# A bidirectional-scan block between two attention blocks, one core: the scan's output projection and the second attention input stage as one pipeline over chunks

## What is computed

```
x  = x + 0.5 * ffn_ref(layernorm(x))                 # attention + experts, first time
x  = x + attn_ref(layernorm(x))                      # the scan block:
        y = scan_forward(..) + scan_reversed(..)     #   (512 channels per token)
        x = base + y @ out_proj_w.T                  #   output stage: 512 -> 256, plus the added row
x  = x + 0.5 * ffn_ref(layernorm(x))                 # second time; its input stage:
        t = (x - mean) / sqrt(var + 1e-5)            #   layernorm, kept for the residual
        a = t * rsqrt(mean(t*t) + 1e-6) * norm_w     #   rmsnorm
        q, k, v = a @ wq.T, a @ wk.T, a @ wv.T       #   256, 64 and 64 columns
```

## Time and profile before

| | |
|---|---|
| median of 3 runs | 8743.57 us (8741.03 to 8743.65) |
| profiled execution, its own time | 8750.53 us |
| its span, first to last instruction | 8748.8 us |
| mean granted TensorE clock | 0.950 of full speed |
| TensorE busy over the span | 84% |
| VectorE busy over the span | 86% |
| first DMA of `mamba_out` | 6207.32 us into the span |
| first q matmul of the second `ffn_in` | 6392.66 us |
| last v matmuls of the second `ffn_in` begin | 6522.91 us |

### The profile page before, as it was taken

The page is one execution under the profiler, slowest core; times in us unless marked ns, Lnnn a source line. Parts: engine busy times, 40 slices in busy tenths (PEclk is TensorE's granted clock), DMA queues, the critical chain, the costliest instruction groups (busy, mean ns, idle before and its releaser), DMA issues. The chain is left out here.

```text
span 8748.8 us, 137191 instructions
## 1 busy us (share of the span) xinstructions
PE 7384.9 (84%) x39098; PEld 2876.4 (33%) x39098; DVE 7557.3 (86%) x11017; ACT 5055.9 (58%) x7663; POOL 3676.0 (42%) x1812
## 2 busy tenths in 40 slices
PE   6788888889997888888878888888777888888799
PEld 3222222225543333333323333333542222222255
DVE  6898888878867999999979999999358988888888
ACT  3577777762235666666655555555224777777622
POOL 0010011100006999999969999999300100110000
PEclk8799999999999999999999999999987999999999
DMA  6001001012262222222223333333561011011122
GB/s 171 17 19 20 19 19 26 19 42 77 72 210 88 83 83 82 82 83 84 83 92 100 102 103 100 100 102 100 171 189 17 19 20 19 19 21 23 42 67 67
DMA packets 554170, 623.35 MB, mean 71 GB/s; under 512 B 205376, under 2 KB 363328, under 8 KB 549408
## 3 DMA queue, kind: packets, MB, share of 16 engines
q1 hardware_dynamic: 548896, 581.63, 22.8%
q0 software_dynamic: 4608, 33.56, 1.9%
HBM read 416.65 MB, written 163.76 MB: 66 GB/s over the span
## 5 line engine op out<-in xcount | busy, mean ns | idle before, releaser
L833 DVE TENSOR_REDUCE ffn_att_mx<-psum 128x1 f32<-128x512 f32 (+2 forms) x4840 | 2915.6, 655 | 389.7 <-PE psum L666 197.4
L794 ACT ACTIVATE ffn_att_e<-psum,unscale 128x1024 f32<-128x1024 f32 (+3 forms) x2560 | 2384.0, 983 | 843.9 <-PE psum L739 842.9
L632 POOL TENSOR_SCALAR_AFFINE_SELECT ffn_att_e<-ffn_att_e 128x512 f32<-128x512 f32 x512 | 324.6, 634 | 3125.8 <-ACT ffn_att_e L794 3125.8
L666 PE MATMUL psum<-ffn_att_k,ffn_att_q 48*128 48x512 f16 (+3 forms) x5384 | 989.1, 368 | 611.2 <-DVE ffn_att_mx L833 545.2
L1628 POOL TENSOR_TENSOR scan_r_h<-scan_r_h,scan_r_cs 128x1024 f32<-128x1024 f32 x512 | 1207.1, 2447 | 148.0 <-ACT scan_r_state L1791 144.7
L705 PE MATMUL psum<-ffn_att_e,ffn_att_v 128*32 128x512 f32 (+3 forms) x10240 | 1248.5, 558 | 10.0 <-issue 3.8
L1628 POOL TENSOR_TENSOR scan_f_h<-scan_f_h,scan_f_cs 128x1024 f32<-128x1024 f32 x512 | 1204.4, 2444 | 118.8 <-ACT scan_f_state L1791 116.1
L1707 PE MATMUL psum<-scan_f_h,ident 128*128 128x512 f32 x2048 | 989.0, 623 | 84.0 <-POOL scan_f_h L1628 83.1
L1707 PE MATMUL psum<-scan_r_h,ident 128*128 128x512 f32 x2048 | 975.0, 617 | 78.1 <-POOL scan_r_h L1628 77.5
L1831 ACT ACTIVATE psum<-scan_r_dt,scan_r_an 128x512 f32<-128x512 f32 x1024 | 698.1, 682 | 456.2 <-DVE scan_r_h L1923 456.0
L1831 ACT ACTIVATE psum<-scan_f_dt,scan_f_an 128x512 f32<-128x512 f32 x1024 | 697.6, 681 | 423.8 <-DVE scan_f_h L1923 423.3
(11 more groups left out here) (240 smaller groups left out, 9216.5 us busy)
## 6 DMA issues: line engine op xcount, KB each, us to landing
scan_f_cs<-scan_f_bcd SPq DMA_DIRECT2D x264, 256.0 KB, 3.2
scan_r_cs<-scan_r_bcd SPq DMA_DIRECT2D x264, 256.0 KB, 3.3
scan_f_bs<-scan_f_bcd SPq DMA_DIRECT2D x82, 256.0 KB, 3.5
scan_r_bs<-scan_r_bcd SPq DMA_DIRECT2D x82, 256.0 KB, 3.5
scan_f_win<-xp SPq DMA_DIRECT2D x18, 1036.0 KB, 6.6
scan_r_win<-xp SPq DMA_DIRECT2D x18, 1036.0 KB, 7.0
ffn_att_q<-q_parts SPq DMA_DIRECT2D x144, 128.0 KB, 2.9
mamba_out_ys<-yz SPq DMA_DIRECT2D x18, 1024.0 KB, 7.3
```

Source lines behind the costliest of these rows:

```text
L632: nc.gpsimd.affine_select(out=part, in_=part, compare_op=ALU.is_ge, fill=0.0, base=0, pattern=[[0, REP], [1, P]], channel_multiplier=-1).t ...
L666: ins = nc.tensor.matmul(psum[:, turns[hh], j * w:(j + 1) * w], q[at, i // HALF, pair, i % HALF * P:(i % HALF + 1) * P], k[at, c * P:c * P ...
L794: nc.scalar.activation(E[:, s % PB, 2 * hp:2 * hp + 2, off:CH], psum[:, 2 * hp:2 * hp + 2, off:CH], ACT.Exp, scale=unscale[:, 0:1]).then_i ...
L833: nc.vector.reduce_max(mx[:, hh * 2 + pairs[0]:hh * 2 + pairs[1], i // HALF, i % HALF, c // TT], psum[:, turn, 0:(pairs[1] - pairs[0]) * w ...
```

## The change

`mamba_out` is removed, and the second call of `ffn_in` with it. A new function `mamba_out_ffn_in` does the work of both in one phase. The first call of `ffn_in` is as before. In the new phase the added rows are written into `xs` and go on from there to the statistics; they are still stored to `x2`, which `ffn_out` reads, and no longer loaded by the input stage. TensorE does out_project(i+2) between q(i) and turn(i+1), into PSUM banks 6 and 7 for even and odd chunks alike. VectorE does join(i+2) and statistics(i+2) between the q remainder and the k remainder of chunk i; ScalarE takes root(i+2) at the end of its step, no longer before the k copy. SP loads `wo` first. Its first DMAs of a step are the store of `t`(i+1), then behind both halves of join(i+2) the store of the rows and the loads of chunk i+4, then the stores of q, k and v. The steps 14 and 15 have no out_project and no join.

```diff
-def mamba_out(nc, tag, psum, y_in, base, x_out, outT, n_chunks):
+def mamba_out_ffn_in(nc, tag, psum, ident, spread, y_in, base, outT, x_out, t_out, qp, kp, v_out, w_norm, wqT, wkT, wvT, B, S):
...
+                def load(i, par):
+                    sp.dma_start(ys[par][:, :, :], cols(y_in, i)).then_inc(loaded[par], 16)
+                    sp.dma_start(bs[par][:, :, :], rows(base, i)).then_inc(loaded[par], 16)
...
+                sp.dma_start(wo[:, :, :], outT.rearrange("(m p) n -> p m n", p=P)).then_inc(wo_in, 16)
+                load(0, 0)
+                load(1, 1)
...
+                for i in range(2):
+                    sp.wait_ge(joined, 2 * (i + 1))
+                    store_x(i, i)
+                    load((i + 2) % n_chunks, i)
+                    if i == 0:
+                        sp.wait_ge(t_ready, TT)
+                        store_t(0, 0)
...
+                    if nxt:
+                        sp.wait_ge(t_ready, TT * (i + 2))
+                        store_t(i + 1, 1 - par)
+                    if more:
+                        sp.wait_ge(joined, 2 * (i + 3))
+                        store_x(i + 2, par)
+                        load((i + 4) % n_chunks, par)
+                    sp.wait_ge(high, 2 * (i + 1))
+                    store_part(0)
+                    sp.wait_ge(v_ready, i + 1)
+                    sp.dma_start(rows(v_out, i), vs[par][:, :, :]).then_inc(stored[par], 16)
+                    sp.wait_ge(low, 2 * (i + 1))
+                    store_part(1)
...
+                def join(i, par):
+                    dve.wait_ge(loaded[par], 32 * (i // 2 + 1))
+                    dve.wait_ge(x_stored[par], 16 * (i // 2))
+                    for n in range(2):
+                        dve.wait_ge(o_ps, 2 * i + n + 1)
+                        nc.vector.tensor_tensor(xs[par][:, 2 * n:2 * n + 2, :], psum[:, 6 + n, :].rearrange("p (t c) -> p t c", t=2),
+                                                bs[par][:, 2 * n:2 * n + 2, :], ALU.add).then_inc(joined, 1)
...
+                def statistics(i, par):
+                    dve.wait_ge(joined, 2 * (i + 1))
...
+                join(0, 0)
+                statistics(0, 0)
+                norm(0, 0)
+                join(1, 1)
+                statistics(1, 1)
+
+                def step(i, par, nxt, more):
+                    if nxt:
+                        norm(i + 1, 1 - par)
+                    split_low_q(i, par)
+                    if more:
+                        join(i + 2, par)
+                        statistics(i + 2, par)
+                    split_low_k(i, par)
...
+                def out_project(i, par):
                     pe.wait_ge(loaded[par], 32 * (i // 2 + 1))
-                    pe.wait_ge(added, 2 * i)
+                    pe.wait_ge(joined, 2 * i)
                     for t in range(TT):
                         for m in range(DM):
-                            ins = nc.tensor.matmul(psum[:, 2 * par + t // 2, (t % 2) * C:(t % 2 + 1) * C],
+                            ins = nc.tensor.matmul(psum[:, 6 + t // 2, (t % 2) * C:(t % 2 + 1) * C],
                                                    ys[par][:, m, t * P:(t + 1) * P], wo[:, m, :], start=m == 0, stop=m == DM - 1)
...
+                out_project(0, 0)
+                out_project(1, 1)
+                turn(0)
+                pe.wait_ge(w_in, 64)
+
+                def step(i, par, nxt, more):
+                    pe.wait_ge(aT_sb, CK * (i + 1))
+                    pe.wait_ge(low, 2 * i)
...
+                    ins.then_inc(q_ps, 1)
+                    if more:
+                        out_project(i + 2, par)
+                    if nxt:
+                        turn(i + 1)
...
-        mamba_out(nc, "mamba_out", psum, yz, base, x2, m["outT"], N)
-        ffn("ffn2", x2, out)
+        mamba_out_ffn_in(nc, "mamba_out_ffn2_in", psum, ident, spread, yz, base, m["outT"], x2, t, qp, kp, v,
+                         f["norm1"], f["wqT"], f["wkT"], f["wvT"], B, S)
+        attend("ffn2", x2, out)
```

More of the change, by code:

```diff
@@ L1942, in mamba_out @@
         ys = [sb(f"ys{p}", [P, DM, CH]) for p in range(2)]
         bs = [sb(f"bs{p}", [P, TT, C]) for p in range(2)]
-        res = sb("res", [P, TT, C])
         wo = sb("wo", [P, DM, C])
-        w_in, loaded = sem("w_in"), [sem("loaded_even"), sem("loaded_odd")]
-        o_ps, added, stored = sem("o_ps"), sem("added"), sem("stored")
-        def phase_steps(eng, step):
-            with eng.Fori(0, n_chunks // 2) as j:
-                for par in range(2):
-                    step(j * 2 + par, par)
+        wn = sb("wn", [P, CK])
@@ L1954, in mamba_out @@
+        high, low, v_ready = sem("high"), sem("low"), sem("v_ready")
+        stored = [sem("stored_even"), sem("stored_odd")]
+        def phase_steps(eng, step):
+            if n_chunks > 2:
+                with eng.Fori(0, n_chunks // 2 - 1) as j:
+                    step(j * 2, 0, True, True)
+                    step(j * 2 + 1, 1, True, True)
+            step(n_chunks - 2, 0, True, False)
+            step(n_chunks - 1, 1, False, False)
         with nc.Block() as block:
@@ L1956, in _ @@
             def _(sp):
[L1957 to L1967, removed]
@@ L1968, in _, with store_x @@
-                phase_steps(sp, step)
-                sp.wait_ge(stored, 16 * n_chunks)
-                for par in range(2):
-                    sp.wait_ge(loaded[par], 32 * (n_chunks // 2 + 1))
+                def load(i, par):
+                    sp.dma_start(ys[par][:, :, :], cols(y_in, i)).then_inc(loaded[par], 16)
+                    sp.dma_start(bs[par][:, :, :], rows(base, i)).then_inc(loaded[par], 16)
+                def store_x(i, par):
+                    sp.dma_start(rows(x_out, i), xs[par][:, :, :]).then_inc(x_stored[par], 16)
@@ new lines, in _, with root, weigh, step @@
+                phase_steps(pe, step)
+            @block.scalar
+            def _(act):
+                act.wait_ge(w_in, 64)
+                def root(i):
+                    act.wait_ge(inv_vars, i + 1)
+                    act.wait_ge(a_ready, TT * i)
+                    nc.scalar.activation(rs[:, :, :], rq[:, :, :], ACT.Sqrt).then_inc(roots, 1)
+                def weigh(i, par):
+                    act.wait_ge(aT_ps, i + 1)
+                    if not (isinstance(i, int) and i < 2):
+                        act.wait_ge(v_ps, i - 1)
+                    for k in range(CK):
+                        nc.scalar.activation(aT[par][:, k, :], psum[:, k, :], ACT.Copy, scale=wn[:, k:k + 1]).then_inc(aT_sb, 1)
+                root(0)
+                weigh(0, 0)
+                root(1)
+                def step(i, par, nxt, more):
+                    act.wait_ge(q_ps, i + 1)
+                    act.wait_ge(stored[par], STORES * (i // 2))
+                    nc.scalar.activation(q2[par][:, 0, :, :], psum[:, 2:4, :], ACT.Copy, scale=spread[:, 0:1]).then_inc(high, 1)
+                    if nxt:
+                        weigh(i + 1, 1 - par)
+                    act.wait_ge(k_ps, i + 1)
+                    nc.scalar.activation(k2[par][:, 0, :], psum[0:KW, 4, :], ACT.Copy, scale=spread[0:KW, 1:2]).then_inc(high, 1)
+                    act.wait_ge(v_ps, i + 1)
+                    nc.scalar.activation(vs[par][:, :, :], psum[:, 5, 0:TT * KW].rearrange("p (t n) -> p t n", n=KW),
+                                         ACT.Copy).then_inc(v_ready, 1)
+                    if more:
+                        root(i + 2)
+                phase_steps(act, step)
```

124 lines of the change are left out of this document (108 added, 16 removed).

## The result

The changed kernel took 8677.87 us in the median of four runs (8676.65 to 8685.46), the kernel before 8743.61 us in four beside them (8741.03 to 8756.33). The ratio is 0.9919, 95% interval 0.9904 to 0.9935: a gain of about 71 us, between 57 and 84; the two medians differ by 65.7 us. A repeat (e1) gave 0.9922 (0.9906 to 0.9939). Over all runs on record the means are 8745.7 us (61 runs of before) and 8678.5 us (8 runs of the changed kernel), 67.2 apart. I had forecast 57.9 us and 8677 to 8699.

The account below looks back on a forecast made before the run. TensorE work took most of the two phases' 315.6 us, beside 25.6 us of waits and 38.7 us of ramps. Now 9.1 + 20.5 + 214.6 + 13.5 = 257.7 us, gaining 57.9: 8686 us, range 8677 to 8699.

Parts of the forecast that it names:

- everything else in the program is untouched: Outside the two joined phases: nothing changes there, so only their rows were read and 57.9 us taken off the whole time.
- The step of 15.33 us: Steady step of the joined stage: a chain through VectorE, from q start to q start, takes 15.33 us, 14 times.
- TensorE idle 0.3 us in it: Steady step: VectorE's order binds, so TensorE with 15.03 us of its own work idles 0.3 us before q.
- TensorE binds: Rival for the steady step: hand-overs and statistics 0.3 us shorter, step 15.03 us, 4.2 us less, 8681.5 us; 15%.
- Start: Stage's first DMA to first out_project: 9.1 us with wo loaded first, needing 2.0 MB landed instead of 3.5 MB.
- fill: From the first out_project matmul to q(0): 20.5 us, through out_project(1), statistics, norm, turn and weighing.
- the last two steps: Steps 14 and 15, without a projection, up to the start of v: 8.15 and 5.35 us, together 13.5 us.
- The moved root: root(i+2) behind the v copy, in time for the turn: priced at nothing; without that cover 0.5 us a step.
- The DMA share: DMA engines in the steady step: 11.0 of 15.33 us, a share of 0.72, no more than before.
- A pause behind the addition: Rival: statistics start later after the addition, by up to 0.69 us; at half, step 15.68 us, time 8690.6 us; 7%.
- The transfers: Rival: late loads or SP's order keep the step at 17.28 us, giving back 27.3 us, 8713 us; 15%.
- The clock: Rival: TensorE at its lower clock level in the joined stage, 8896 us if in all steps; 3%.

Follow-up runs that it names:

- e3: The changed kernel with half of the v matmuls of the joined stage left out, VectorE's order unchanged: 8685.19 us in one run, step 15.09 us.
- e2: The changed kernel with VectorE taking the k remainder of chunk i ahead of statistics(i+2): 8673.17 us, ratio 0.9919 to the kernel before, step 15.06 us.
- e12: The changed kernel with the base rows loaded a second time per chunk into a tile that nothing reads: 8688.61 us in one run, step 15.09 us.
- e8: The changed kernel with the loads of a chunk issued one step later, behind the first stores of q and k: 8803.52 us in one run, step 25.1 us.
- e6: The kernel before, only mamba_out edited: four buffer sets, earlier loads, none redundant, TensorE one chunk further ahead of the additions: 8690.64 us in one run.

## What of the prediction held, and which step failed

**The step that failed** is the opening one, "everything else in the program is untouched", and with it the sum that takes 57.9 us "off either" time. The code outside the stage is untouched; its duration is not. By the means of the times the gain is 67.2 us: the 57.9 of the forecast, 4.7 more inside the stage, and 4.6 outside it, where the prediction had nothing (8.4 by the ratio's 71). The stage's 62.6 us alone would have made 8681.0 us, within the range; what lies outside carried the time by the ratio below it. Over all kernels with another stage that part is 4 to 10 us, from 61 runs of before and 36 of the others; it most likely lies in the second attention, and its cause is open. One profile of before could not show it. That its execution was 7 us over the median, which I spread "over the whole span", is no safe hint: the changed kernel's profiled execution was 7.6 us over its median too.

**The step of 15.33 us** was the mis-sized term inside the stage. It is 15.09, so 14 of them are 3.3 us shorter, most of the 4.7. The second addition starts 0.11 earlier (7.10 instead of 7.21). The hand-over of 0.1 from the addition to the statistics is 0.04, the statistics and the remainder behind them 2.87 instead of 3.00, because the remainder doesn't wait for the last reciprocal as I had chained it. The last hand-over is 0.13 instead of 0.1. The k remainder was named rightly as the link in which q waits (e3), but with 0.03 us of margin over TensorE's own 15.06, not 0.3. So "TensorE idle 0.3 us in it" is wrong, and the rival *TensorE binds* is right but for that margin (e2): 8681.5 us was its time. The path was right, and the two limits lie closer than forecast.

**The other terms.** Start 8.3 us for 9.1 (its bounds reached down to 7.7), fill 19.8 for 20.5, the last two steps 13.6 for 13.5, sum 253.0 for 257.7. The moved root costs nothing while its cover stands, and e2 shows 1.35 us in step 14 once it comes late. The DMA share is 0.76 for 0.72.

**A pause behind the addition** doesn't exist. The addition begins at 6264.45 and lasts 0.69, the statistics that read its rows begin at 6265.18, 0.04 behind its end. The rule of the Trainium skill (VectorE: DVE Perf Modes, section "The DRAIN you can't avoid") would set 0.42 us there (0.69 less 0.266; the prediction wrote 0.43). The trace disagrees if the rule is read as time behind the shown duration; whether a flush lies inside the 0.69 us no run here shows.

**The transfers** don't hold the step. TensorE waits for none after the first, and 17% more bytes in the same time (264 GB/s for 226) leave it at 15.09 us (e12). Their lead does matter: with loads issued only behind k's copy, 8.5 us before the projection can start on them, the kernel is slower than before (e8). **The clock** in the stage is 1.00 from the first q on (0.88 in the fill), and the row after a 6.95 us wait shows what the rival would have cost: 8.84 us for 7.07.

**Where the gain is from** is the part in which the prediction's account was incomplete. It booked 53.2 us on joining. e6 has 44.7 of the 62.6 us with two separate phases, loads early enough and a looser wait for the additions; joining itself is worth the boundary, 17.9 us. The changed kernel gets the early load as well, since its lead is 22 us.

## What to carry to other kernels

Before two phases are joined, first ask each one's waits how late their loads are asked for: deeper buffers, loads without waste and a looser wait gave 44.7 of 62.6 us here, and only the boundary's 17.9 needed the joining. In a pipelined step, sum each candidate chain from start to start, TensorE's own first; where two lie within a few tenths, the forecast is the larger of both and the error is that of the small pieces (here the hand-overs, 0.04 us within VectorE and 0.13 from VectorE to TensorE, and two links that came out 0.1 shorter). And profile the kernel before more than once: a difference of 8 us in another stretch of the program is not the edit's until its spread over executions is known.

## What was not expected of the hardware

The same 12821 matmuls of the second attention took 1718 to 1752 us in 17 profiles, at a granted clock of 0.95 to 0.92, with no other engine's busy time differing by more than 2.1 us. In the steps 0 to 13 of the joined stage the clock was 1.00 in all profiles but e8's (0.85).

SP's time to issue one DMA is not constant. In the changed kernel's timeline, two issues of SP:

```profile
6256.81 3.10 SPq L2017 DMA_DIRECT2D q_parts<-mamba_out_ffn_in_q  x2
...
6265.95 0.39 SPq L1988 DMA_DIRECT2D mamba_out_ffn_in_ys<-yz  x1
```

The pair of q stores, right behind the other stores of q, k and v, takes 3.10 us to issue, the load nine us later 0.39. Why is not shown. Nothing waited for it here, since the loads have 22 us of lead.
